# A chunked recurrence cut into two halves of eight heads, with unread products for TensorE

## Chip, cores and metric

The kernel runs on one core of a Trainium2 chip. The metric is the device time of one execution in microseconds (us), the median of several.

## The reference

Two layers, each a recurrent attention and a feed-forward part, on 2 sequences of 1024 tokens with 512 features. The change touches only the attention of the second layer, a test-time-training recurrence over 16 heads of 32 features, in chunks of 16 tokens:

```python
def step(S, inp):                       # S: (B, H, 32, 32), 64 chunks one after the other
    qi, ki, vi, ei = inp
    kh = einsum('bchd,bhde->bche', ki, S)
    target = vi - ki
    mu = mean(kh, -1); rstd = rsqrt(var(kh, -1) + EPS)
    kh_hat = (kh - mu) * rstd
    g = w * kh_hat + b - target
    gw = g * w
    v_new = (gw - mean(gw, -1) - kh_hat * mean(gw * kh_hat, -1)) * rstd
    A = where(tri, einsum('bchd,bshd->bhcs', qi, ki), 0) * ei
    qh = einsum('bchd,bhde->bche', qi, S) - einsum('bhcs,bshe->bche', A, v_new)
    o = qi + _ln(qh, w, b)
    S = S - einsum('bchd,bche->bhde', ki * ei, v_new)
    return (S, o)
```

## The kernel before

The program runs in stages, each closed by a barrier of all engines: the first layer's recurrence, its feed-forward part with the second layer's projections, then `ttt_recurrence` (the stage of the change), attention output, shared experts, routed experts, last stage.

`ttt_recurrence` runs 64 steps (`STEPS`), one for each chunk. All 16 heads and both sequences are done in each: partitions hold 2 sequences x 4 heads x 16 tokens, and the free dimension holds 4 groups `g` of 4 heads. Everything is in float32. In step n:

- TensorE multiplies the next keys (L1343) and these queries (L1350) with the state `S`. It then waits for `u` (the update v_new, scaled) and adds the correction `cross` x `u` to the next keys' product (L1388, so that the next step need not wait for the new state), updates the state in its PSUM bank (L1393), and adds `am` x `u` to the queries' product (L1399). `prepare` (L1357) makes the raw products of keys with queries and with the next keys.
- ScalarE squares the keys' product, takes the root, and copies `S`, `cross` and the result `qh` out of PSUM.
- VectorE does the normalisation and its derivative, a chain of 14 operations that ends in `u` (L1326), then `ub` (L1329, `u` by sequence) and `am` (L1332, masked).
- SP loads the keys and queries (`KQ`), goals (`te`) and keys by row (`kk`) of 8 steps at a time into two buffers, and stores `qh`. GpSimd only clears tiles.

Each engine runs its own order, and semaphores tie them. A float32 matmul stands in the trace as two records, so a block of 8 products has 16.

Of the kernel before, what the change touches and what calls it, by code (L numbers as in the profile page):

```python
# [6 lines left out]
ALU = mybir.AluOpType  # L7
# [6 lines left out]
P = 128  # L14
# [1136 lines left out]
def ttt_recurrence(nc, K, bank, a):  # L1151
# [7 lines left out]
    bS, bQ, bA, bC = bank[0:4]  # L1159
    bH = bank[4:6]  # L1160
    G = KC
# [3 lines left out]
    zero = ph.sb("zero", [P, 2 * P])  # L1165
# [6 lines left out]
    u, ub = ph.sb("u", [P, G, DH]), ph.sb("ub", [P, G, B, DH])  # L1172
    c1, c2, c3, c4, c5, c6 = (ph.sb(f"c{k}", [P, G, DH]) for k in range(6))
    eps, m, re = ph.sb("eps", [P, 1]), ph.sb("m", [P, 6, G]), ph.sb("re", [P, G])
    s = {n: nc.alloc_semaphore(name=f"ttt_{n}") for n in (
        "consts", "zero", "eps", "w2", "s0", "S", "KH", "KS", "QS", "A", "KK", "cross", "sq", "s2", "sd", "xw", "r1", "v1", "rs", "re",
# [13 lines left out]

    def rows(name, i):
        return a[name][i * B * P:(i + 1) * B * P, :]

    with nc.Block() as block:
        @block.sync
        def _(sp):
# [3 lines left out]
            def load(i):  # L1200
                f = i % 2
                if i >= 2:
                    sp.wait_ge(s["QS"], ST * (i - 1))
                    sp.wait_ge(s["KK"], ST * (i - 1))
# [5 lines left out]
                if i >= 2:  # L1210
                    sp.wait_ge(s["u"], ST * (i - 1))
                    sp.wait_ge(s["SU"], ST * (i - 1))
# [8 lines left out]
            def store(i):  # L1221
                sp.wait_ge(s["qh"], ST * (i + 1))
# [20 lines left out]

        @block.scalar
        def _(act):
            nc.scalar.preload_act_table_set("sqrt_and_others")

            def deviation(n):
                act.wait_ge(s["KH"], n + 1)
                if n:  # L1250
                    act.wait_ge(s["r2"], n)
                nc.scalar.activation(c2[:].rearrange("p g e -> p (g e)"), bH[n % 2][:, 0:P], ACT.Square).then_inc(s["sq"], 1)
                act.wait_ge(s["s2"], n + 1)
                nc.scalar.activation(m[:, 2], m[:, 1], ACT.Sqrt, scale=1.0 / DH, bias=eps[:, 0:1]).then_inc(s["sd"], 1)

            def state(n):
                act.wait_ge(s["SU"], n)
                if n:
                    act.wait_ge(s["QS"], n)
                    act.wait_ge(s["KS"], n + 1)  # L1260
                else:
                    act.wait_ge(s["s0"], 1)
                nc.scalar.copy(S[:].rearrange("p g b e -> p (g b e)"), bS[:, 0:2 * P]).then_inc(s["S"], 1)

            state(0)
            act.wait_ge(s["eps"], 1)
            deviation(0)
            for n in range(STEPS):
                f, r = place(n)
                if n + 1 < STEPS:  # L1270
                    act.wait_ge(s["KK"], n + 1)
                    act.wait_ge(s["KH"], n + 1)
# [3 lines left out]
                act.wait_ge(s["AU"], n + 1)  # L1276
                if r == 0 and n >= 2 * ST:
                    act.wait_ge(qh_out[f], 16 * 8 * (n // (2 * ST)))
                nc.scalar.copy(qh[f][:, r].rearrange("p g e -> p (g e)"), bQ[:, 0:P]).then_inc(s["qh"], 1)

        @block.vector
        def _(dve):
            nc.vector.memset(eps[:], 1e-6).then_inc(s["eps"], 1)
# [4 lines left out]
            def over_e(t):  # L1288
                return t.unsqueeze(2).to_broadcast([P, G, DH])

            for n in range(STEPS):
                f, r = place(n)
                kh = bH[n % 2][:, 0:P].rearrange("p (g e) -> p g e", g=G)
                dve.wait_ge(s["sq"], n + 1)
                nc.vector.tensor_reduce(m[:, 1], c2[:], AX, ALU.add).then_inc(s["s2"], 1)
                nc.vector.tensor_tensor(c3[:], kh, w2[:], ALU.mult).then_inc(s["xw"], 1)
                dve.wait_ge(s["xw"], n + 1)
                nc.vector.tensor_reduce(m[:, 4], c3[:], AX, ALU.add).then_inc(s["r1"], 1)
                dve.wait_ge(s["r1"], n + 1)
                nc.vector.scalar_tensor_tensor(c4[:], over_e(m[:, 4]), -1.0 / DH, c3[:], ALU.mult, ALU.add).then_inc(s["v1"], 1)  # L1300
                dve.wait_ge(s["sd"], n + 1)
                nc.vector.reciprocal(m[:, 3], m[:, 2]).then_inc(s["rs"], 1)
                dve.wait_ge(s["v1"], n + 1)
                dve.wait_ge(s["rs"], n + 1)
                nc.vector.tensor_tensor(c3[:], c4[:], over_e(m[:, 3]), ALU.mult).then_inc(s["t"], 1)
                nc.vector.tensor_tensor(c1[:], kh, over_e(m[:, 3]), ALU.mult).then_inc(s["hat"], 1)
                if r == 0:
                    dve.wait_ge(in_te[f], 16 * 16 * (n // (2 * ST) + 1))
                dve.wait_ge(s["t"], n + 1)
                nc.vector.tensor_tensor(c3[:], c3[:], te[f][:, r, :, 0:DH], ALU.add).then_inc(s["gw"], 1)  # L1310
                nc.vector.tensor_tensor(re[:], m[:, 3], te[f][:, r, :, DH], ALU.mult).then_inc(s["re"], 1)
                dve.wait_ge(s["hat"], n + 1)
                dve.wait_ge(s["gw"], n + 1)
                nc.vector.tensor_tensor(c2[:], c3[:], c1[:], ALU.mult).then_inc(s["p"], 1)
                dve.wait_ge(s["p"], n + 1)
                nc.vector.tensor_reduce(m[:, 5], c2[:], AX, ALU.add).then_inc(s["r2"], 1)
                dve.wait_ge(s["r2"], n + 1)
                nc.vector.tensor_tensor(c5[:], c1[:], over_e(m[:, 5]), ALU.mult).then_inc(s["q"], 1)
                dve.wait_ge(s["q"], n + 1)
                nc.vector.scalar_tensor_tensor(c6[:], c5[:], 1.0 / DH, c3[:], ALU.mult, ALU.subtract).then_inc(s["v2"], 1)  # L1320
                if n:
                    dve.wait_ge(s["SU"], n)
                    dve.wait_ge(s["AU"], n)
                dve.wait_ge(s["re"], n + 1)
                dve.wait_ge(s["v2"], n + 1)
                nc.vector.tensor_tensor(u[:], c6[:], over_e(re[:]), ALU.mult).then_inc(s["u"], 1)  # L1326
                dve.wait_ge(s["u"], n + 1)
                if n + 1 < STEPS:
                    nc.vector.tensor_tensor(ub[:], u[:].unsqueeze(2).to_broadcast([P, G, B, DH]),  # L1329
                                            seq[:].unsqueeze(1).unsqueeze(3).to_broadcast([P, G, B, DH]), ALU.mult).then_inc(s["ub"], 1)  # L1330
                dve.wait_ge(s["A"], n + 1)
# [1134 lines left out]
```

## Time and profile before

| | us |
|---|---|
| median of 3 runs | 2649.17 (2643.64 to 2650.5) |
| the profiled execution | 2673.8 |
| its span | 2672.0 |
| mean granted TensorE clock | 0.886 |
| TensorE busy | 2250.8 (84%) |
| VectorE busy | 1544.7 (58%) |
| ScalarE busy | 1116.9 (42%) |
| GpSimd busy | 861.7 (32%) |

The span goes from the first to the last instruction. PE is TensorE's matmul, PEld its weight load, DVE VectorE, ACT ScalarE, POOL GpSimd, SP the queue that issues transfers. PEclk is the clock that TensorE is granted, as a share of 2.4 GHz: 0.50 is 1.2 GHz. Busy shares are averages over stages with different limits, so the recurrence is read by itself.

### The profile page before, as it was taken

To read this page: it belongs to the slowest core of one execution; us is meant where nothing else is said; L and a number is where in the kernel's file an instruction comes from. 1 tells how busy PE (TensorE), PEld (TensorE's weight loads), DVE (VectorE), ACT (ScalarE), POOL (GpSimd) and SP (SyncE) were. 2 spreads that over 40 slices of the span, in tenths; PEclk is the share of its full clock that TensorE was granted. 3 is DMA by queue.
4 is the path that set the end of the run, shared out by engine and by line. 5 is a ranking of instruction groups with operands and counts; after the bars stand their busy time and mean duration, and the time that the engine had idled before them with its cause. 6 is when DMAs were issued, how large, how long until landed. Compare 5 with 4: busy or idle time off the path is not lost. (4 is left out here: it accounts for less than half of the span.)

```text
span 2672.0 us, 59064 instructions
## 1 busy us (share of the span) xinstructions
PE 2250.8 (84%) x23684; PEld 1946.7 (73%) x23684; DVE 1544.7 (58%) x3549; ACT 1116.9 (42%) x2103; POOL 861.7 (32%) x666
## 2 busy tenths in 40 slices
PE   7999983999994999994678994999999999999930
PEld 6778762777773889893446773999999899999930
DVE  4545553555542766666957633656655556655658
ACT  4334332555552322222441111555555555555523
POOL 0000000122211000003410476656665656666621
PEclk9999995888885876777999996999999999999965
DMA  2111103344448354333530002234235523233147
GB/s 106 39 38 38 39 22 118 138 168 178 176 154 205 92 159 105 92 95 117 173 124 12 1 2 94 64 134 140 79 136 190 196 89 139 88 130 133 40 172 284
DMA packets 154572, 300.44 MB, mean 112 GB/s; under 512 B 67097, under 2 KB 93209, under 8 KB 139645
## 3 DMA queue, kind: packets, MB, share of 16 engines
q1 hardware_dynamic: 108285, 181.71, 21.2%
q0 software_dynamic: 44480, 115.41, 12.7%
q8 instruction: 139, 2.28, 0.4%
q10 hardware_dynamic: 1616, 0.62, 0.1%
q14 instruction: 52, 0.43, 0.1%
HBM read 296.72 MB, written 106.27 MB: 151 GB/s over the span
## 5 line engine op out<-in xcount | busy, mean ns | idle before, releaser
L91 PE MATMUL bank<-routed_xh,routed_guh 128*128 128x256 f32 (+1 forms) x1536 | 437.7, 285 | 29.3 <-DVE routed_xl L2171 29.3
L92 PE MATMUL bank<-routed_xh,routed_gul 128*128 128x256 f32 (+1 forms) x1536 | 437.0, 284 | 0.0
L93 PE MATMUL bank<-routed_xl,routed_guh 128*128 128x256 f32 (+1 forms) x1536 | 434.9, 283 | 0.0
L2205 DVE TENSOR_TENSOR routed_gul<-routed_guf,routed_guh 128x2816 fp32r<-128x2816 f32 x64 | 197.9, 3092 | 250.7 <-ACT routed_guh L2148 250.7
L91 PEld LDWEIGHTS bank<-routed_xh,routed_guh 128*128 128x128 f32 (+1 forms) x1536 | 280.5, 183 | 37.7 <-issue 35.3
L2089 POOL DMA_INDIRECT routed_x<-mid_x,routed_xi x132 | 276.5, 2095 | 55.9 <-issue 53.5
L92 PEld LDWEIGHTS bank<-routed_xh,routed_gul 128*128 128x128 f32 (+1 forms) x1536 | 280.2, 182 | 2.0
L93 PEld LDWEIGHTS bank<-routed_xl,routed_guh 128*128 128x128 f32 (+1 forms) x1536 | 281.6, 183 | 0.0
L2098 POOL DMA_INDIRECT mid_y<-routed_y,routed_yi x132 | 138.9, 1052 | 246.7 <-ACT routed_y L2164 224.1
L2158 ACT CAST routed_ih<-routed_sil 128x256 fp32r<-128x256 f32 (+1 forms) x192 | 78.0, 406 | 240.4 <-DVE routed_sil L2210 240.4
L2148 ACT CAST routed_guh<-routed_guf 128x2816 fp32r<-128x2816 f32 x64 | 163.5, 2555 | 35.7 <-DMA routed_guf<-in_GU,routed_wi 35.6
L91 PE MATMUL bank<-routed_dnh,routed_ih 128*128 128x512 f32 (+1 forms) x384 | 157.0, 409 | 0.0
L1887 POOL DMA_INDIRECT mid_slots<-moe_pair,moe_slot x96 | 100.6, 1048 | 173.5 <-DVE moe_slot L1814 144.5
L92 PE MATMUL bank<-routed_dnh,routed_il 128*128 128x512 f32 (+1 forms) x384 | 151.0, 393 | 0.0
L93 PE MATMUL bank<-routed_dnl,routed_ih 128*128 128x512 f32 (+1 forms) x384 | 150.4, 392 | 0.0
L325 POOL TENSOR_TENSOR gla_xt<-gla_xt,gla_shift 128x512 f32<-128x512 f32 x16 | 20.2, 1263 | 342.6 <-DMA gla_xt<-in_x 319.8
L1477 POOL MEMSET out_eps<- 128x1 f32 x1 | 0.1, 98 | 401.2 <-POOLq L83 401.2
L2216 DVE TENSOR_TENSOR routed_il<-routed_sil,routed_ih 128x256 fp32r<-128x256 f32 (+1 forms) x192 | 82.7, 431 | 60.4 <-ACT routed_ih L2158 60.4
L2213 DVE TENSOR_TENSOR routed_dnl<-routed_dnf,routed_dnh 128x1536 fp32r<-128x1536 f32 x64 | 112.2, 1753 | 4.4 <-ACT routed_dnh L2156 4.4
L2164 ACT COPY routed_y<-bank 128x512 f32<-128x512 f32 x128 | 74.3, 588 | 85.9 <-PE bank L93 85.8
L2171 DVE TENSOR_TENSOR routed_xl<-bank,routed_xh 128x512 fp32r<-128x512 f32 x130 | 83.8, 686 | 34.8 <-ACT routed_xh L2135 34.8
L1357 PE MATMUL bank<-ttt_KQ 128*64 128x64 f32 x2032 | 100.4, 273 | 0.0
(456 smaller groups left out, 5780.5 us busy)
## 6 DMA issues: line engine op xcount, KB each, us to landing
last_y<-mid_y SPq DMA_DIRECT2D x16, 1536.0 KB, 9.7
mid_ks<-ffn_kT SPq DMA_DIRECT2D x16, 1024.0 KB
mid_qs<-ffn_qT SPq DMA_DIRECT2D x16, 1024.0 KB
ttt_KQ<-mid_ks SPq DMA_DIRECT2D x16, 1024.0 KB, 6.9
ttt_KQ<-mid_qs SPq DMA_DIRECT2D x16, 1024.0 KB, 12.0
mid_te<-ffn_te SPq DMA_DIRECT2D x16, 264.0 KB, 4.1
ttt_te<-mid_te SPq DMA_DIRECT2D x64, 66.0 KB, 6.0
gla_xT<-in_xT SPq DMA_DIRECT2D x16, 256.0 KB, 3.2
```

Source lines behind the costliest of these rows:

```text
L91: pe.matmul(out, hi(c), whi(c), start=start and c == 0, stop=False, skip_group_check=True)
L92: pe.matmul(out, lo(c), whi(c), start=False, stop=False, skip_group_check=True)
L93: last = pe.matmul(out, hi(c), wlo(c), start=False, stop=stop and c == n - 1, skip_group_check=True)
L1357: last = pe.matmul(out[half(b), g * R64:(g + 1) * R64], keys(n, g, b), other(g, b), start=True, stop=True, skip_group_check=True)
L1887: nc.gpsimd.indirect_dma_start(a["slots"], bass.IndirectOffsetOnAxis(ap=slot6[:, n, j:j + 1], axis=0), pair[:, n, j], None).then_inc(given ...
L2089: nc.gpsimd.indirect_dma_start(x[q][:, h], None, a["x3"], bass.IndirectOffsetOnAxis(ap=xi[q][:, h:h + 1], axis=0)).then_inc(x_in[q], 16)
L2098: nc.gpsimd.indirect_dma_start(a["y"], bass.IndirectOffsetOnAxis(ap=yi[q][:, h:h + 1], axis=0), y[q][:, h], None, bounds_check=B * L * TOP ...
L2148: nc.scalar.copy(guh[q][:].rearrange("p a c n -> p (a c n)"), guf[q][:]).then_inc(s["guh"].sem, 1)
L2171: last = nc.vector.tensor_tensor(xl[q][:, c].rearrange("p c t -> p (c t)"), t_bank[k][:], xh[q][:, c].bitcast(F32).rearrange("p c t -> p ( ...
L2205: nc.vector.tensor_tensor(gul[q][:].rearrange("p a c n -> p (a c n)"), guf[q][:], guh[q][:].bitcast(F32).rearrange("p a c n -> p (a c n)") ...
L2213: nc.vector.tensor_tensor(dnl[r][:].rearrange("p c n -> p (c n)"), dnf[r][:], dnh[r][:].bitcast(F32).rearrange("p c n -> p (c n)"), ALU.su ...
L2216: nc.vector.tensor_tensor(il[r][0:m, c], sil[k][0:m], ih[r][0:m, c].bitcast(F32), ALU.subtract).then_inc(s["il"].sem, 1)
```

## The change

The 4 groups of a step are cut into two halves `h` of 2 groups (eight heads). Every operation of a step is done for each half, with semaphores, PSUM banks and tiles for each. VectorE's order is written out in `both`: the second part of one half's chain takes turns with the first part of the other half's. The product `ub` moves from VectorE to GpSimd. The copies that shared the tiles `c1` to `c6` have tiles of their own, `u` and `ub` are doubled, and the products of keys with next keys go behind the queries' product in its bank.

TensorE gets products that nobody reads, of zeros with zeros in float32r: two of 512 columns that open the state banks, one that opens `bA[0]`, 40 of 512 columns ahead of the wait for the first `KQ`, 8 behind it, and one of 384 columns in each half step between the keys' correction and the state update. They add zeros to banks or parts of banks.

```diff
-    bS, bQ, bA, bC = bank[0:4]
-    bH = bank[4:6]
-    G = KC
+    HALVES, G = 2, KC
+    GH = G // HALVES
+    bS, bQ, bH, bA = bank[0:2], bank[2:4], bank[4:6], bank[6:8]
+    AFTER_Q = GH * DH
...
+            def by_sequence(n, h):
+                pool.wait_ge(done["u"][h], n + 1)
+                nc.gpsimd.tensor_tensor(ub[n % 2][:, heads(h)], u[n % 2][:, heads(h)].unsqueeze(2).to_broadcast([P, GH, B, DH]),
+                                        seq[:].unsqueeze(1).unsqueeze(3).to_broadcast([P, GH, B, DH]), ALU.mult).then_inc(done["ub"][h], 1)
...
             for n in range(STEPS):
-                f, r = place(n)
-                if n + 1 < STEPS:
-                    act.wait_ge(s["KK"], n + 1)
-                    act.wait_ge(s["KH"], n + 1)
-                    nc.scalar.copy(cross[:].rearrange("p g n -> p (g n)"), bC[:, 0:G * R64]).then_inc(s["cross"], 1)
-                    deviation(n + 1)
-                    state(n + 1)
...
+                for h in range(HALVES):
+                    if n + 1 < STEPS:
+                        deviation(n + 1, h)
+                        state(n + 1, h)
+                    result(n, h)
+                    if n + 2 < STEPS:
+                        next_keys(n + 1, h)
...
+            def both(n, h, m, k):
+                to_goal(n, h)
+                rates(n, h)
+                along_keys(n, h)
+                masked(n, h)
+                along_summed(n, h)
+                if m < STEPS:
+                    squares_summed(m, k)
+                projected(n, h)
+                if m < STEPS:
+                    weighted(m, k)
+                taken_off(n, h)
+                if m < STEPS:
+                    weighted_summed(m, k)
+                update(n, h)
+                if m < STEPS:
+                    weighted_centred(m, k)
+                    inverse(m, k)
+                    keys_normed(m, k)
+                    weighted_normed(m, k)
+
+            first_of(0, 0)
+            for n in range(STEPS):
+                both(n, 0, n, 1)
+                both(n, 1, n + 1, 0)
...
+            def prepare(n, h):
                 if n + 1 < STEPS:
+                    if n:
+                        pe.wait_ge(done["qh"][h], n)
...
+            def unread(out, width, n):
+                for _ in range(n):
+                    pe.matmul(out[:, D - width:], still[:, 0:P], still[:, 0:width], start=False, stop=False, skip_group_check=True)
+
+            pe.wait_ge(s["still"], 1)
+            for h in range(HALVES):
+                pe.matmul(bS[h][:], still[:, 0:P], still[:], start=True, stop=False, skip_group_check=True).then_inc(s["s0"], 1)
+            pe.matmul(bA[0][:], still[:, 0:P], still[:], start=True, stop=False, skip_group_check=True)
+            unread(bA[0], D, 40)
             pe.wait_ge(in_KQ[0], 16 * 4)
+            unread(bA[0], D, 8)
+            for h in range(HALVES):
+                keys_times_state(0, h)
+                pe.matmul(bH[h][:, 0:GH * DH], zero[:, 0:P], zero[:, 0:GH * DH], start=False, stop=True, skip_group_check=True).then_inc(done["KH"][h], 1)
+                prepare(0, h)
+            keys_times_state(1, 0)
+            queries_times_state(0, 0)
             for n in range(STEPS):
...
+                for h in range(HALVES):
+                    pe.wait_ge(done["u"][h], n + 1)
+                    if n + 1 < STEPS:
+                        keys_corrected(n + 1, h)
+                        unread(bS[h], D - GH * B * DH, 1)
+                        state_updated(n, h)
+                    queries_corrected(n, h)
+                    m, k = n + h, 1 - h
+                    if m + 1 < STEPS:
+                        keys_times_state(m + 1, k)
+                    if m < STEPS:
+                        queries_times_state(m, k)
+                    if n + 1 < STEPS:
+                        prepare(n + 1, h)
```

## Rows read from the trace of the kernel before

**Rows 1.** The page, part 2: granted TensorE clock in tenths, 40 slices.

```profile
PEclk9999995888885876777999996999999999999965
```

**Rows 2.** Table by stretches of the recurrence; columns are in its first line.

```profile
core 0: us, PE busy (x) PEld busy (x) DVE busy (x) ACT busy (x) POOL busy (x), PEclk, DMA share, GB/s
...
874.00:964.00 90.00, 81.39 (x1820) 76.94 (x1818) 72.27 (x282) 28.18 (x89) 0.00 (x0) 0.92 0.51 128
964.00:997.00 33.00, 33.00 (x485) 31.71 (x482) 18.64 (x71) 6.71 (x21) 0.00 (x0) 0.51 0.31 88
...
1003.00:1037.00 34.00, 34.00 (x488) 32.58 (x489) 20.57 (x80) 7.65 (x24) 0.00 (x0) 0.51 0.24 30
```

**Rows 3.** Timeline, TensorE alone, one step at 1.2 GHz: start, duration, line.

```profile
1013.78 1.01 PE L1343 MATMUL bank<-ttt_S,ttt_KQ 128*64 128x32 f32 x16
1014.60 1.05 PE L1350 MATMUL bank<-ttt_S,ttt_KQ 128*64 128x32 f32 x16
1015.58 1.07 PE L1388 MATMUL bank<-ttt_u,ttt_cross 64*64 64x32 f32 x16
1016.58 1.97 PE L1393 MATMUL bank<-ttt_ub,ttt_kk 128*128 128x64 f32 x8
1018.47 1.07 PE L1399 MATMUL bank<-ttt_u,ttt_am 64*64 64x32 f32 x16
1019.47 1.97 PE L1357 MATMUL bank<-ttt_KQ 128*64 128x64 f32 x32
1021.23 1.01 PE L1343 MATMUL bank<-ttt_S,ttt_KQ 128*64 128x32 f32 x16
```

**Rows 4.** Timeline, TensorE in one step at 2.4 GHz.

```profile
930.22 0.66 PE L1388 MATMUL bank<-ttt_u,ttt_cross 64*64 64x32 f32 x16 [0.61 <-DVE ttt_u L1326]
...
930.81 1.10 PE L1393 MATMUL bank<-ttt_ub,ttt_kk 128*128 128x64 f32 x8
...
935.10 0.66 PE L1388 MATMUL bank<-ttt_u,ttt_cross 64*64 64x32 f32 x16 [0.61 <-DVE ttt_u L1326]
```

**Rows 5.** Timeline, VectorE and ScalarE in that step.

```profile
931.24 0.29 DVE L1295 TENSOR_REDUCE ttt_m<-ttt_c 128x4 f32<-128x128 f32 x1 [0.27 <-ACT ttt_c L1252]
931.44 0.28 DVE L1296 TENSOR_TENSOR ttt_c<-bank,ttt_w 128x128 f32<-128x128 f32 x1
931.55 0.30 ACT L1254 ACTIVATE ttt_m<-ttt_m,ttt_eps 128x4 f32<-128x4 f32 x1 [0.35 <-DVE ttt_m L1295]
...
933.17 0.16 DVE L1311 TENSOR_TENSOR ttt_re<-ttt_m,ttt_te 128x4 f32<-128x4 f32 x1
...
935.08 0.42 DVE L1329 TENSOR_TENSOR ttt_ub<-ttt_u,ttt_seq 128x256 f32<-128x256 f32 x1
```

**Rows 6.** Timeline, the first steps and the last u.

```profile
843.12 0.64 PE L1350 MATMUL bank<-ttt_S,ttt_KQ 128*64 128x32 f32 x16
...
849.32 0.29 DVE L1310 TENSOR_TENSOR ttt_c<-ttt_c,ttt_te 128x128 f32<-128x128 f32 x1 [6.29 <-DMA ttt_kk<-mid_kk]
...
851.09 0.29 DVE L1326 TENSOR_TENSOR ttt_u<-ttt_c,ttt_re 128x128 f32<-128x128 f32 x1
...
851.43 1.07 PE L1388 MATMUL bank<-ttt_u,ttt_cross 64*64 64x32 f32 x16 [7.68 <-DVE ttt_u L1326]
...
1223.05 0.29 DVE L1326 TENSOR_TENSOR ttt_u<-ttt_c,ttt_re 128x128 f32<-128x128 f32 x1
```

**Rows 7.** Timeline, products of 512 columns at 1.2 GHz, ahead of this stage.

```profile
404.27 0.63 PE L92 MATMUL bank<-gla_Wo_hi,gla_yTl 128*128 128x512 f32 x1
404.70 0.63 PE L93 MATMUL bank<-gla_Wo_lo,gla_yTh 128*128 128x512 f32 x1
```

**Rows 8.** Groups of instructions by form, GpSimd: busy us, mean ns.

```profile
L833 POOL TENSOR_TENSOR ffn_te<-ffn_te,ffn_tm 128x512 f32<-128x512 f32 x16 | 16.8, 1048 | 41.8 <-DVE ffn_tm L1033 41.8
...
L820 POOL TENSOR_TENSOR ffn_te<-ffn_kw 128x16 f32<-128x16 f32 x16 | 3.6, 223 | 0.0
```

**Rows 9.** Timeline, TensorE where the clock rises.

```profile
993.16 1.97 PE L1357 MATMUL bank<-ttt_KQ 128*64 128x64 f32 x32
...
996.68 0.65 PE L1388 MATMUL bank<-ttt_u,ttt_cross 64*64 64x32 f32 x16
```

More of the change, by code:

```diff
@@ L1311, in _ @@
[L1311 to L1318, printed above, removed]
@@ L1354, in keys_times, with of, column, keys_times_state @@
-            def keys_times(out, n, other, made):
-                for g in range(G):
+            def of(h):
+                return range(h * GH, (h + 1) * GH)
+            def column(g, width):
+                return slice(g % GH * width, (g % GH + 1) * width)
+            def keys_times_state(n, h):
+                pe.wait_ge(done["S"][h], max(n, 1))
+                if n:
+                    pe.wait_ge(done["hat"][h], n)
+                for g in of(h):
+                    for b in range(B):
+                        last = pe.matmul(bH[h][half(b), column(g, DH)], keys(n, g, b), S[:, g, b, :],
+                                         start=(g == h * GH), stop=False, skip_group_check=True)
+                last.then_inc(done["KS"][h], 1)
@@ new lines, in queries_times_state @@
+            def queries_times_state(n, h):
+                if n + 1 < STEPS:
+                    pe.wait_ge(done["cross"][h], n + 1)
+                else:
+                    pe.wait_ge(done["qh"][h], n)
+                for g in of(h):
+                    for b in range(B):
+                        last = pe.matmul(bQ[h][half(b), column(g, DH)], queries(n, g, b), S[:, g, b, :],
+                                         start=(g == h * GH), stop=False, skip_group_check=True)
+                last.then_inc(done["QS"][h], 1)
@@ L1356, in keys_times @@
+            def keys_times(out, n, h, other, made):
+                for g in of(h):
                     for b in range(B):
-                        last = pe.matmul(out[half(b), g * R64:(g + 1) * R64], keys(n, g, b), other(g, b),
+                        last = pe.matmul(out[half(b), column(g, R64)], keys(n, g, b), other(g, b),
                                          start=True, stop=True, skip_group_check=True)
-                last.then_inc(s[made], 1)
-            def prepare(n):
-                keys_times(bA, n, lambda g, b: queries(n, g, b), "A")
+                last.then_inc(done[made][h], 1)
@@ L1404, in ttt_recurrence, with keys_corrected @@
-    nc.clear_and_free_semaphores([*s.values(), *cleared, *in_KQ, *in_te, *qh_out])
+                    keys_times(bQ[h][:, AFTER_Q:AFTER_Q + GH * R64], n, h, lambda g, b: keys(n + 1, g, b), "KK")
+                keys_times(bA[h], n, h, lambda g, b: queries(n, g, b), "A")
+            def keys_corrected(n, h):
+                pe.wait_ge(done["cross"][h], n)
+                for g in of(h):
+                    for b in range(B):
+                        last = pe.matmul(bH[h][half(b), column(g, DH)], cross[half(b), g, :], u[(n - 1) % 2][half(b), g, :],
+                                         start=False, stop=True, skip_group_check=True)
+                last.then_inc(done["KH"][h], 1)
```

229 lines of the change are left out of this document (122 added, 107 removed).

## Prediction

> **What bounds the kernel now.** I read the page first. The granted clock falls between full and half speed in the slices of 67 us that hold the chunked recurrence [rows 1]. So I cut that stage (about 839 to 1224 us) into stretches of like clock. The reader is to see in [rows 2] that there are two regimes and little between. Where the clock is 0.50 to 0.51, TensorE is busy all of the time (33.00 of 33.00 us, 34.00 of 34.00 us) and VectorE 56 to 60% of it. Where it is 0.92, VectorE is busy 80% and TensorE 90%. I then read one step of each kind. At 0.50 (1.2 GHz) a step is 1021.23 - 1013.78 = 7.45 us, with six TensorE blocks back to back and no wait [rows 3]: TensorE bounds it. At 1.00 (2.4 GHz) a step is 935.10 - 930.22 = 4.88 us, and TensorE waits 0.61 us for u in it [rows 4]. There the bound is the loop u, correction product, Square on ScalarE, the chain of VectorE operations that [rows 5] shows parts of, u again.
>
> From u of step 0 to u of step 63 there are 1223.05 - 851.09 = 371.96 us, or 5.904 us a step [rows 6]. With 4.88 and 7.45 as the two kinds, (5.904 - 4.88) / 2.57 = 0.40 of the steps, 25 of 63, run at 1.2 GHz. So the clock in this stage is worth more (25 x 2.57 = 65 us) than anything that can be hidden at full clock, and the question of the change is which regime it is in.
>
> **The change part by part.** *TensorE's blocks* are cut in two, with the same products in sum. From the starts in [rows 3], at 1.2 GHz: key product with S 0.82, query product with S 0.98, correction by cross 1.00, state update 1.89, query correction 1.00, `prepare` 1.76, in sum 7.45 us. Half a step is 3.72 us.
>
> *The unread product of 384 columns* has no row before. The nearest is a product of 512 columns of the same kind at 1.2 GHz, 404.70 - 404.27 = 0.43 us from start to start [rows 7]; by columns that is 0.43 x 384 / 512 = 0.32 us. Bounds: 0.1 us if most of its stream covers the weight loads around it (the weight load column is as busy as the product column in [rows 2]), 0.55 us if it also exposes a weight load of 0.23 us, which is one product's pitch in the state update (1.89 / 8, [rows 3]). I take 0.32 us, since TensorE's blocks stand back to back and nothing is there to hide it. A half step at 1.2 GHz is then 3.72 + 0.32 = 4.04 us, and a step 8.1 us; I take 8.15 for waits at twice as many seams, with 7.65 and 8.6 as ends.
>
> *VectorE* gets 30 operations a step in place of 16 less ub, half as wide, two chains in turn. An operation of 128 elements takes 0.29 us and lets the next independent one start after 0.20 (931.24 to 931.44, [rows 5]). One of 4 elements takes 0.16 us. So one of 64 takes about 0.22 us. Its pitch lies between 0.13 us (0.20 less 64 elements at the 128-element rate) and 0.20 us. By the lower end, with the 128-wide mask at 0.20, a half step is about 2.2 us, by the upper 3.0 us. At 1.2 GHz both lie under TensorE's 4.04 us and cost nothing.
>
> *ub moves to GpSimd.* A tensor_tensor there takes 0.22 us for 16 elements and 1.05 for 512 [rows 8], so about 0.4 us for 128. It starts when u ends, and TensorE has the correction (0.5 us at 1.2 GHz) and the unread product before it needs ub. Hidden at 1.2 GHz; at 2.4 GHz those two are some 0.3 ((930.81 - 930.22) / 2, [rows 4]) and 0.16 us, so up to 0.1 us may show in a half step. VectorE loses 0.42 us a step [rows 5]. The Trainium skill ("SBUF — State Buffer", section "Who interferes with whom") says that a VectorE instruction with two SBUF inputs and a GpSimd one that reads SBUF lock each other out. By that ub could be late by one VectorE operation more; no row here shows the pair overlapping, and the sum does not use it.
>
> *ScalarE* goes from five operations a step to ten. The one to watch is its order: Square, then the wait for the sum of squares, Sqrt, and behind these the state copy, the result copy and the copy of cross, for all of which TensorE waits (`prepare` for the result). The loop is sum of squares, Sqrt, state copy, result copy, `prepare` of this half, correction of the other half, Square, sum of squares. A ScalarE operation takes about 0.3 us (Sqrt 0.30, [rows 5]), a VectorE one 0.25 with its hand-over, `prepare` of a half 1.76 / 4 = 0.44 at 2.4 GHz and the half correction 0.3 + 0.1 until its reader starts. That makes 0.25 + 3 x 0.3 + 0.44 + 0.4 + 0.3 = 2.3 us a half step, and TensorE's own work is (4.88 - 0.61) / 2 + 0.16 = 2.3 us. With VectorE's 2.2 to 3.0 that makes 2.45 us a half step, 4.9 a step at 2.4 GHz (4.6 to 6.0). That is no better than 4.88: the two halves overlap what was serial, but everything has become as long as the step. At 1.2 GHz its two TensorE terms double, to 3.1 us, under the 4.04.
>
> *SP's queue* only waits on two semaphores for one; its loads are issued eight steps ahead, and nothing else stands behind them.
>
> *The 48 unread products ahead of the first step.* 40 (and 3 that open banks) run after the zeros are there, 8 after KQ has landed. They delay the first key product by at most 8 x 0.43 = 3.4 us, which is hidden: TensorE finishes its work ahead of the loop near 844 us [rows 6], while VectorE can't go on until the last `kk` rows land at 849.3, and u of step 0 is at 851.09. That same wait takes away what they are for. TensorE now runs out of work at about 843.8 and starts again at 851.4; the clock is 0.50 there although it was 1.00 before the pause (843.12: 16 products in 0.64 us; 851.43: 1.07 us). The loads are not changed, so with the new kernel it stands idle at least 4 us at this place and, as here, begins the loop at 1.2 GHz.
>
> **Does the clock rise again?** In the kernel before it does at 996.6, after `prepare` and both products with S had run in one stretch from 993.16; the correction at 996.68 already takes 0.65 us in place of 1.07 [rows 3, 9]. In this stretch a product of 64 columns goes by every 0.055 us (1.76 / 32, [rows 3]); in the state update it is one every 0.24 us, in the corrections one of 32 columns on a quarter of the array every 0.06 us. The same run in the step of 1019.47 brought no rise, so it does not bring one each time. After the change the run is half as long (16 + 8 + 8 products, 1.8 us), and a correction, the state update and a correction stand between two of them. What is added is the unread product, 0.32 us of full-array work in 4.04. It adds to the mean, but it does not replace the long run after which the clock rose. I choose between "rises after some steps" and "never rises" by the row that it is nearest to, the stretches at 0.50 in which TensorE worked all the time [rows 2], and expect the whole loop at 0.50.
>
> **Sum.** 63 x 8.15 = 513.5 against 371.96: +141.5 us. The second half of the last step adds about 2. Nothing else in the program changes. 2673.8 + 143.5 = 2817 us against the profiled execution (span 2672.0 and 1.8 around it). That execution is 24.6 us over the median of 2649.17. If its excess lies elsewhere, the median after is 2793; if it lies in this stage's share of 1.2 GHz, it is 2817. I say 2800; own range 2770 to 2840.
>
> **Rivals.**
> A, the forecast: 1.2 GHz in the whole loop, 2800 us. Chance 0.70.
> B, full clock for (nearly) the whole loop, faster. Place: the first steps after the pause at 851. It decides at a single rise: at 2.4 GHz a half step of 2.45 us leaves no pause of note where there now is one of 0.61 [rows 4], so a clock that has risen may well stay up. One rise in 128 half steps suffices. Price: 63 x 4.9 = 309, -63 us; 2673.8 - 63 = 2611 or, from the median, 2586: 2600 us. For it: the added full-array products; against it: the broken dense run. The Trainium skill ("TensorE: Matmul & The Clock Gate", section "What's actually happening") says that sustained activity releases the throttle; read as busy time, it would give this rival. The trace here speaks against that reading: 33 us and 34 us fully busy at 0.50 to 0.51 [rows 2]. Chance 0.20.
> C, alternating as now, 0.4 of the steps at 1.2 GHz: 0.4 x 8.15 + 0.6 x 4.9 = 6.2 us a step, +19 us: 2668 us. For it: it is what the kernel does now; against it: that the halves make the work even, so that it should stay on one side. Chance 0.07.
> D, full clock, but VectorE's 30 operations at the upper pitch bind at 2 x 3.0 = 6.0 us a step: +6 us, 2655. Chance 0.03.
>
> **How the numbers follow.** A measurement of this kernel tells 0.3% (8 us) from no change. Slower by more: A and most of C, 0.76. Within: D and a little of C, 0.04. Faster: B, 0.20. The predicted time is A's. For 8 in 10 the range must reach into B, since A alone holds 0.7. It goes from 2595, within B, to 2830, a little under A's own end; that leaves out about half of B and a few hundredths of A.
>
> **What would show it.** Right: PEclk 5 in all slices of the recurrence, half steps of about 4.05 us with TensorE always busy, the unread product at a pitch of 0.3 us, VectorE about half busy, ub never waited for; 851 us for the first correction, with a pause ahead of it. Wrong: a rise of the clock after the pause, seen as correction blocks of 8 in 0.3 us; the clock then staying at 1.00; or no pause, should `kk` land earlier. If half steps at 2.4 GHz are much over 2.5 us, the chain on ScalarE (`prepare` behind the result copy) or VectorE's pitch was mis-sized.

## The result, and the profile after it

| | before | after |
|---|---|---|
| median (4 runs each) | 2649.84 us (2643.64 to 2651.82) | 2854.91 us (2850.90 to 2862.91) |
| profiled execution, its span | 2673.8 us, 2672.0 | 2862.91 us, 2861.1 |
| granted clock over the span | 0.886 | 0.829 |
| u of step 0 to last u | 371.96 us | 555.3 us |

The changed kernel is slower: 1.0782 times the time, 95% interval 1.0752 to 1.0812. That is 205 us, where +150 was forecast. Of the profiled difference of 189.1 us the loop holds 183.3; u of step 0 comes 2.8 us later, and from the last u to the end takes 2.9 us more. Here and below, a ratio and its interval leave out executions more than 1.5% above the fastest of the same kernel; medians and ranges hold all of them.

The page after, the granted clock in 40 slices, beside [rows 1]:

```profile
PEclk9999977988975555555589999699999999999975
```

The table by stretches, beside [rows 2]:

```profile
core 0: us, PE busy (x) PEld busy (x) DVE busy (x) ACT busy (x) POOL busy (x), PEclk, DMA share, GB/s
...
852.00:900.00 48.00, 45.85 (x543) 42.14 (x543) 27.20 (x177) 13.61 (x54) 4.39 (x11) 0.50 0.44 105
900.00:1000.00 100.00, 100.00 (x1216) 91.69 (x1215) 53.02 (x340) 28.55 (x113) 9.18 (x23) 0.50 0.33 69
...
1300.00:1400.00 100.00, 100.00 (x1203) 91.80 (x1205) 53.53 (x343) 28.71 (x114) 9.19 (x23) 0.50 0.06 10
```

There is one regime where there were two: 0.50 from end to end, TensorE busy for 100.00 of 100.00 us, VectorE 53%. How the loop begins, from the timeline (start, duration, engine), beside [rows 6]:

```profile
832.70 13.19 PE L1496 MATMUL bank<-ttt_still 128*128 128x512 f32 x48
...
848.45 0.41 PE L1450 MATMUL bank<-ttt_S,ttt_KQ 128*64 128x32 f32 x8
...
852.50 0.23 DVE L1356 TENSOR_TENSOR ttt_gw<-ttt_t,ttt_te 128x64 f32<-128x64 f32 x1 [4.32 <-DMA ttt_kk<-mid_kk]
853.88 0.21 DVE L1380 TENSOR_TENSOR ttt_u<-ttt_v,ttt_re 128x64 f32<-128x64 f32 x1
...
854.15 0.64 PE L1474 MATMUL bank<-ttt_u,ttt_cross 64*64 64x32 f32 x8 [5.29 <-DVE ttt_u L1380]
```

The 48 unread products end at 845.8, and the last work ahead of the loop still runs warm (four float32 products, eight records, in 0.41 us). Then TensorE stands idle for 5.29 us, because VectorE waits 4.32 us for the `kk` load, and the first correction takes 0.64 us: half speed. One half step of the loop, TensorE alone, beside [rows 3]:

```profile
1100.92 0.64 PE L1474 MATMUL bank<-ttt_u,ttt_cross 64*64 64x32 f32 x8
...
1101.49 0.69 PE L1496 MATMUL bank<-ttt_still 128*128 128x384 f32 x1
...
1101.97 0.95 PE L1482 MATMUL bank<-ttt_ub,ttt_kk 128*128 128x64 f32 x4
1102.85 0.64 PE L1490 MATMUL bank<-ttt_u,ttt_am 64*64 64x32 f32 x8
...
1103.42 0.64 PE L1439 MATMUL bank<-ttt_S,ttt_KQ 128*64 128x32 f32 x8
...
1103.87 0.62 PE L1450 MATMUL bank<-ttt_S,ttt_KQ 128*64 128x32 f32 x8
1104.30 1.10 PE L1457 MATMUL bank<-ttt_KQ 128*64 128x64 f32 x16
...
1105.33 0.64 PE L1474 MATMUL bank<-ttt_u,ttt_cross 64*64 64x32 f32 x8
```

No block has an idle time ahead of it. The half step is 4.41 us here and 555.3 / 127 = 4.373 on the mean, where 4.04 (4.075 with its share for waits) was forecast. The first and the last interval between two u are shorter (2.33 and 3.03 us), so the steady half step is the 4.41; steps are compared by it below. The other engines do the waiting. The chain of waits from 860 to 1400 us has none of TensorE (waited for: us in total, times, longest):

```profile
POOL ttt_ub L1257 <- DVE ttt_u L1380: 492.5, 123, 4.0
DVE ttt_am L1384 <- PE bank L1457: 192.2, 122, 1.6
ACT ttt_cross L1291 <- PE bank L1457: 154.2, 122, 1.3
```

The groups of instructions give ub on GpSimd 399 ns (forecast 0.4 us), and the list of u's line gives its first and last start, the measure of the loop used below:

```profile
L1257 POOL TENSOR_TENSOR ttt_ub<-ttt_u,ttt_seq 128x128 f32<-128x128 f32 x126 | 50.3, 399 | 517.9 <-DVE ttt_u L1380 517.9
```

```profile
L1380 DVE TENSOR_TENSOR ttt_u<-ttt_v,ttt_re x128: 211/215/225, 853.9 to 1409.2; 128x64 f32<-128x64 f32 x128
```

### The profile page after: what moved, and what is told of

It is laid out like the page before. It is cut to its first block and busy times, and to the rows that moved or that the text cites. A ratio compares the mean times of both kernels' runs of the same rounds, so it can differ in the third digit from the quotient of the medians.

```text
span 2861.1 us, 60552 instructions
## 1 busy us (share of the span) xinstructions
PE 2475.9 (87%) x23861; PEld 2139.0 (75%) x23861; DVE 1585.1 (55%) x4447; ACT 1176.8 (41%) x2422; POOL 910.0 (32%) x792
## 5 line engine op out<-in xcount | busy, mean ns | idle before, releaser
L1257 POOL TENSOR_TENSOR ttt_ub<-ttt_u,ttt_seq 128x128 f32<-128x128 f32 x126 | 50.3, 399 | 517.9 <-DVE ttt_u L1380 517.9
L1384 DVE TENSOR_TENSOR ttt_am<-bank,ttt_tri 128x128 f32<-128x128 f32 x128 | 37.3, 291 | 196.7 <-PE bank L1457 196.7
L1457 PE MATMUL bank<-ttt_KQ 128*64 128x64 f32 x2032 | 139.2, 317 | 0.0
L1482 PEld LDWEIGHTS bank<-ttt_ub,ttt_kk 128*128 128x128 f32 x504 | 136.0, 332 | 0.0
L1457 PEld LDWEIGHTS bank<-ttt_KQ 128*64 128x64 f32 x2032 | 123.8, 226 | 0.1
L1482 PE MATMUL bank<-ttt_ub,ttt_kk 128*128 128x64 f32 x504 | 119.5, 393 | 0.0
```

The source lines that it names most:

```text
L1457: last = pe.matmul(out[half(b), column(g, R64)], keys(n, g, b), other(g, b), start=True, stop=True, skip_group_check=True)
L1482: last = pe.matmul(bS[h][:, column(g, B * DH)], kk[f][:, r, g].rearrange("p j d -> p (j d)"), ub[n % 2][:, g].rearrange("p b e -> p (b e)" ...
```

## The experiments

They were made in three groups, each on a chip of its own with runs of the kernel before on it: 2651.75 us (12 runs), 2650.13 (11) and, for e9 to e12, 2717.25 (29). On the third chip what lies behind the loop is some 60 us longer (1507.6 to 1513.2 us from the last u to the end, 1449.0 in the first profile), and the loop isn't. So times are compared within a group, and loops across them.

The questions are three. Why does the clock stay down? What does a half step cost at either level? What are the unread products worth?

### e1: fill the pause ahead of the first step

```diff
@@ behind the last product ahead of the loop
+            unread(bS[1], D - GH * B * DH, 36)
```

> The changed kernel with 36 more unread products of 384 columns on TensorE between its last product ahead of the loop and the wait for the first u, so that the 5.3 us pause there is filled. Theory (the clock at which the loop is entered decides, and then stays): the loop begins at 2.4 GHz and the granted clock is 1.00 in all of it; half steps of 2.3 to 2.6 us, so 126 of them take 290 to 328 us in place of 555, and the kernel takes 2590 to 2640 us. Rival 1 (half steps in turns cannot hold 2.4 GHz, however they begin): the clock falls within some steps and the time stays at 2830 to 2870. Rival 2 (the clock alternates as in the kernel before): 2650 to 2750.

Measured: 2786.14 us (2752.59 to 2860.83, 4 runs), ratio 1.045 [1.0363, 1.0536]. The profiled execution is the longest of them:

```profile
844.82 4.67 PE L1496 MATMUL bank<-ttt_still 128*128 128x384 f32 x26
851.39 0.54 PE L1474 MATMUL bank<-ttt_u,ttt_cross 64*64 64x32 f32 x8 [1.90 <-DVE ttt_u L1380]
```

The products ended at 849.5, 1.90 us too early; the correction begins warm (0.54 us for the block, which falls to half speed within it), and from there the loop is 555.2 us, all at 0.50, as in the changed kernel. The other three executions are 72 to 108 us shorter, and their mean granted clock is 0.855 to 0.869 where the profiled one has 0.828, so part of their loops must have been at 2.4 GHz (their loops themselves were not seen). The expected 2590 to 2640 was missed: 36 products don't always fill the pause, and even the best execution stays far over a loop at full clock.

### e2: no product in the half steps; e11: no unread product at all

```diff
@@ e2, in the half step
-                        unread(bS[h], D - GH * B * DH, 1)
@@ e11, that line too, and ahead of the loop
-            unread(bA[0], D, 40)
-            unread(bA[0], D, 8)
```

> The changed kernel without the unread product of 384 columns in each half step; the 48 ahead of the loop stay. Theory (entered at 1.2 GHz, the loop stays there with or without the product, and the product only costs time): clock 0.50 in the whole loop; the half step falls from 4.41 us by the product's 0.48 us less what it hid of the next weight load (0.17), to about 4.1 us, so 126 x 0.31 = 39 us off: about 2816 us. If the product hides nothing: 3.93 us, 2795 us. Rival (the sparse product is what keeps the clock from alternating): alternating clock, under 2750 us.

> The two halves without any unread product, ahead or in the loop, but for the three that open banks. Theory (the loop is entered at 1.2 GHz through the pause anyway, and stays): clock 0.50 in the whole loop, half steps of 4.08 us, 2816 us as without the products in the loop. Rival (the 48 products ahead do something for the loop): a time over 5 us away from 2816.

Measured: e2 2816.44 us, e11 2883.4 on the third chip (one run each); their loops are both 515.0 us (u from 856.9 to 1371.9 and from 853.4 to 1368.4), all at 0.50. e2 met the expected 2816. e11 lies 67 us over it, and all of that is behind the loop, which takes 1513.2 us to the end there and 1442.7 in e2. TensorE in e2:

```profile
1102.41 0.64 PE L1474 MATMUL bank<-ttt_u,ttt_cross 64*64 64x32 f32 x8
1102.98 1.11 PE L1482 MATMUL bank<-ttt_ub,ttt_kk 128*128 128x64 f32 x4
1104.02 0.64 PE L1490 MATMUL bank<-ttt_u,ttt_am 64*64 64x32 f32 x8
1104.59 0.64 PE L1439 MATMUL bank<-ttt_S,ttt_KQ 128*64 128x32 f32 x8
...
1106.50 0.64 PE L1474 MATMUL bank<-ttt_u,ttt_cross 64*64 64x32 f32 x8
```

Two things follow. The 48 products ahead of the loop change nothing in it. And the unread product costs 4.41 - 4.09 = 0.32 us a half step at 1.2 GHz, as forecast (by the loops, (555.3 - 515.0) / 127 = 0.317). It stands for 0.48 us in the changed kernel's timeline, but the state update behind it is shorter for it (0.88 us there, 1.04 here). What is left is 2 x 4.09 = 8.18 us a step with the same products as 7.45 in [rows 3]. So 0.73 us a step come from cutting the blocks in half.

### e7: the two corrections side by side

```diff
                     if n + 1 < STEPS:
                         keys_corrected(n + 1, h)
+                    queries_corrected(n, h)
+                    if n + 1 < STEPS:
                         unread(bS[h], D - GH * B * DH, 1)
                         state_updated(n, h)
-                    queries_corrected(n, h)
```

> The changed kernel with the queries' correction directly behind the keys' correction, ahead of the unread product and the state update; nothing is added or left out. In its trace a pair of products follows the last at 0.107 us in a block, but at 0.22 to 0.35 us where the shape of the tile changes (128x64, 64x64, 128x128), four times in a half step. Theory (the change of shape costs this): one change fewer, the half step goes from 4.41 to about 4.29 us, 126 x 0.12 = 15 us less, about 2840 us, at 0.50 throughout. Rival (the waits on semaphores at the blocks' starts cost it): the waits are the same in number, 4.41 us and 2855 us.

Measured: 2830.92 us (one run; 2840 was expected), loop 537.7 at 0.50.

```profile
1102.61 0.64 PE L1474 MATMUL bank<-ttt_u,ttt_cross 64*64 64x32 f32 x8
1103.06 0.62 PE L1490 MATMUL bank<-ttt_u,ttt_am 64*64 64x32 f32 x8
1103.61 0.69 PE L1496 MATMUL bank<-ttt_still 128*128 128x384 f32 x1
1104.09 0.95 PE L1482 MATMUL bank<-ttt_ub,ttt_kk 128*128 128x64 f32 x4
```

The key correction now takes 0.45 us (1102.61 to 1103.06) and not 0.57, with the same four products (eight records). Behind it stands a block of its own tile shape (64\*64, the pair printed after the names) and not one of 128\*128. The loop is 17.6 us shorter, 0.14 us a half step. The waits are all still there, so it isn't they that cost: it is each change of tile shape between one product and the next. Where a wait stands and the shape stays, nothing shows: the two blocks with S follow each other after 0.45 and 0.43 us, the pace of their products. The single records of e2 and e7 say the same: from one pair of records to the next it is 0.100 us within most of a block and equally from block to block where the shape stays, but 0.221 or 0.244 us where it changes, and 0.351 us from the state update, whose own pitch is 0.213 to 0.266, to the next shape. The kernel before has four such changes in a step, the halves without the product have eight, and (8.18 - 7.45) / 4 = 0.18 us each. The Trainium skill ("TensorE: Matmul & The Clock Gate", section "Step-by-step: what each phase is for") says that a weight load is pulled ahead of running products where their row groups don't conflict, or where it goes to the background weight buffer. A change of shape that stands in the way of that could be the reason; no run here separates it from another one.

### e3 and e5: the pause filled, none or one product in the half steps

```diff
@@ e3: 36 in the pause, none in the half step
+            unread(bS[1], D - GH * B * DH, 36)
-                        unread(bS[h], D - GH * B * DH, 1)
@@ e5: 54 in the pause, one in the half step as in the change
+            unread(bS[1], D - GH * B * DH, 54)
```

> The changed kernel with the pause filled by 36 unread products of 384 columns, and without the product in each half step. Theory: TensorE is fed well enough by the half steps themselves, the clock stays at 1.00, and the time is that of the kernel with filled pause or up to 20 us less (126 x 0.16 us at most). Rival (the product in each half step is needed to hold the clock): stretches at 0.50 in the loop, 30 us or more above the kernel with filled pause.

> As the kernel with filled pause, but with 54 products in the pause, since 36 ended 1.9 us before the first u. Theory: the loop now begins at 2.4 GHz; with the product in each half step it stays there longer than without it (which was until a 1.6 us halt of TensorE at 947 us), perhaps to the end: 126 half steps of 2.5 us = 315 us, so about 2600 to 2615 us if it stays. If a halt still ends it, all after that is at 0.50 and the time lies between, by 1.9 us for each half step left. Rival (the clock falls without a halt): falls at places that differ from run to run with no idle time before them.

Measured: e3 2748.26 us (2745.98 to 2827.33, 4 runs), ratio 1.0344 [1.0272, 1.0416]; e5 2762.53 (2759.86 to 2763.69, 4 runs), 1.0409 [1.0362, 1.0457]. TensorE and two stretches of e3, and the like of e5:

```profile
946.27 0.55 PE L1482 MATMUL bank<-ttt_ub,ttt_kk 128*128 128x64 f32 x3
948.43 0.48 PE L1482 MATMUL bank<-ttt_ub,ttt_kk 128*128 128x64 f32 x1 [1.61 <-issue]
...
860.00:947.00 87.00, 86.81 (x1899) 78.79 (x1895) 82.54 (x550) 41.34 (x183) 14.47 (x37) 1.00 0.58 139
949.00:1290.00 341.00, 341.00 (x4350) 310.74 (x4352) 194.81 (x1245) 105.41 (x417) 33.10 (x83) 0.50 0.31 73
```

```profile
1001.02 0.40 PE L1450 MATMUL bank<-ttt_S,ttt_KQ 128*64 128x32 f32 x8
1002.91 0.69 PE L1457 MATMUL bank<-ttt_KQ 128*64 128x64 f32 x16 [1.48 <-issue]
...
1005.00:1300.00 295.00, 295.00 (x3552) 270.75 (x3551) 157.12 (x1006) 84.50 (x335) 26.71 (x67) 0.50 0.27 64
```

This is the run pair that shows both levels in one loop. With the pause filled (in e3 0.53 us of it were left) the halves run at full clock: 2.37 us a half step in e3, 2.55 in e5, TensorE busy 86.81 of 87.00 us. Then TensorE halts, 1.61 or 1.48 us in the middle of its work, with "issue" and no other engine as its releaser (e5 has one more halt, of 0.7 us at 910, behind which the clock stays up). The clock falls to 0.50, and from there it stays at 0.50 for 341 and 295 us of unbroken work. Loops: 448.4 us in e3, 458.3 in e5. The same code runs at either level in one execution, and which one depends on what it came in with. e3's theory (the clock stays at 1.00) failed, and so did its rival: in e5 the product stood in each half step and the clock fell all the same. For e5 its second branch came, a halt and 0.50 from there. One of e3's four executions, 2827.33 us at a mean clock of 0.831, is 79 us longer than the others (0.860 to 0.862); it must have fallen much earlier.

### e8: five products in each half step; e6: a burst in every eighth step

```diff
@@ e8
-                        unread(bS[h], D - GH * B * DH, 1)
+                        unread(bS[h], D - GH * B * DH, 5)
@@ e6, with the 54 of e5 in the pause
-                        unread(bS[h], D - GH * B * DH, 1)
+                        unread(bS[h], D - GH * B * DH, 12 if n % 8 == 7 and h == 0 else 1)
```

> The changed kernel with five unread products of 384 columns in each half step in place of one. At 1.2 GHz that is 4 x 0.32 = 1.28 us more in each, so if the loop stays at 0.50 (rival: what is added cannot bring the clock back) the half step is 5.7 us and the time 2855 + 161 = 3016 us. Theory (it is full-array work in a run that is missing; with enough of it the clock rises within the first steps and stays): clock 1.00, TensorE bounds the half step at 2.4 + 5 x 0.16 = 3.2 us, so 126 x 3.2 = 403 us in place of 555: about 2700 us, faster although more is done.

> As the kernel with the longer fill, but in every eighth step the first half step has 12 unread products of 384 columns in place of one: 8 x 11 x 0.16 to 0.32 us = 14 to 28 us of work more. Theory (dense work brings the clock back, so that a fall costs at most eight steps): the clock is 1.00 in most of the loop, and the time is 2610 to 2650 us, in all runs. Rival (once at 1.2 GHz, the loop stays there whatever is added): as the kernel with the longer fill plus 14 to 28 us.

Measured: e8 2724.97 us (one run); e6 2664.05 (2652.46 to 2698.85, 8 runs), ratio 1.0029 [0.9984, 1.0073]. TensorE in e8, with a stretch of 100 us, and in e6:

```profile
870.43 1.97 PE L1496 MATMUL bank<-ttt_still 128*128 128x384 f32 x5
872.20 0.81 PE L1482 MATMUL bank<-ttt_ub,ttt_kk 128*128 128x64 f32 x4
872.94 0.42 PE L1490 MATMUL bank<-ttt_u,ttt_am 64*64 64x32 f32 x8
...
900.00:1000.00 100.00, 100.00 (x1753) 93.28 (x1750) 72.30 (x462) 39.03 (x154) 12.38 (x31) 1.00 0.47 118
```

```profile
1120.34 3.34 PE L1496 MATMUL bank<-ttt_still 128*128 128x384 f32 x12
1123.52 0.55 PE L1482 MATMUL bank<-ttt_ub,ttt_kk 128*128 128x64 f32 x4
```

e8 does more work than the changed kernel in every half step, with the same kind of pause ahead of the loop (5.93 us idle), and takes 130 us less (about 2700 was expected): after some 20 us at half speed (5.69 us a half step) the clock rises in the state update at 872.20, and the rest of the loop, 418.4 us in all, is at 1.00. In e6 the clock fell after a halt of 1.78 us at 1092, stayed down for some 27 us, and came back within a burst: twelve products in 3.2 us, and the state update behind them already in 0.49. So full-array products do bring the clock back; one of 384 columns in a half step did not in the 295 us of e5. e6's executions missed the 2610 to 2650 expected of all of them, and by its interval it can't be told from the kernel before.

### e12: the pause filled, three in each half step

```diff
@@ with the 54 of e5 in the pause
-                        unread(bS[h], D - GH * B * DH, 1)
+                        unread(bS[h], D - GH * B * DH, 3)
```

> The halves with the longer fill (54 products in the pause) and three products of 384 columns in each half step. Theory (enough to outlast the halts of TensorE of 1.5 to 2 us, which ended 2.4 GHz with none and with one product): clock 1.00 to the end of the loop, half steps of 2.55 + 2 x 0.16 = 2.88 us, 363 us in place of 555: 2640 to 2665 us. Rival (three are not enough to outlast a halt, or to come back from one): 0.50 from some halt on, with half steps of 5.05 us, and 2700 us or more.

Measured: 2732.92 us (2726.16 to 2737.17, 10 runs), ratio 1.0057 [1.0029, 1.0086], loop 368.6 at 1.00 throughout:

```profile
1000.00:1100.00 100.00, 100.00 (x1898) 92.53 (x1894) 80.69 (x517) 43.58 (x173) 13.63 (x34) 1.00 0.52 138
```

A half step is 368.6 / 127 = 2.90 us, the forecast 2.88. (The expected 2640 to 2665 us were meant for a chip that does the kernel before in 2650; 1.0057 times that is 2665.) Held at full clock from end to end, the halves are no faster than the kernel before with its mix of both levels, 0.6% slower by the medians: the products that hold it there cost what it brings, and there is no idle time of TensorE left for them to lie in (100.00 of 100.00 us).

### e4, e9, e10: whole steps with unread products

The kernel before, with 100 products of 256 columns ahead, 62 in the pause, and three (e4), six (e9) or none (e10) in each step just before the wait for u, where [rows 4] have 0.61 us of idle time:

```diff
+            def unread(n):
+                for _ in range(n):
+                    pe.matmul(bank[6][:, 2 * P:], still[:, 0:P], still[:, 0:2 * P], start=False, stop=False, skip_group_check=True)
...
+            unread(100)
...
+                unread(62 if n == 0 else 3)
```

> The kernel before, its steps whole, with the unread products alone: 100 of 256 columns ahead of the first keys, 62 in the pause before the first u, 3 in each step where TensorE waits for u, all into a bank that nothing uses. Theory (clock and halves are separate; the products fill the wait for u of 0.61 us in a 4.88 us step): clock 1.00 in the whole loop, 63 steps of 4.9 us = 309 us in place of 372, so 63 us less: 2585 to 2600 us. Rival (the whole step has a stretch too sparse to hold the clock, whatever the products): alternating clock with steps of 4.9 and 8.1 us, 2640 to 2700 us.

> The kernel before, steps whole, with 100 products ahead, 62 in the pause, and six of 256 columns in the wait for u of each step in place of three. With three its step was 4.88 us at 2.4 GHz, and the profile still showed the clock at 0.50 for 3.4, 13.7 and 34 us, each after a halt of TensorE of 1.2 to 1.8 us. Theory (more full-array work in the step brings the clock back sooner after a halt): fewer or shorter stretches at 0.50, 63 steps of 4.9 to 5.0 us, 2600 to 2625 us. Rival (six no longer fit in the wait and lengthen the step by more than they give back): 2630 to 2660 us.

> The kernel before with the 100 products ahead and the 62 in the pause alone, none in the steps. Theory (the clock of whole steps does not depend on how they were entered, since they lose and regain it by themselves): within 10 us of the kernel before, 2640 to 2655 us. Rival (the clean start is what gave the gain of 23 us): 2620 to 2635 us.

Measured: e4 2628.4 us (2613.39 to 2656.05, 9 runs), ratio 0.9905 [0.9856, 0.9954]; e9 0.9953 [0.9921, 0.9986] (12 runs) and e10 0.9959 [0.9925, 0.9993] (10 runs) on the third chip. All three gains are under 2%, but their intervals lie below 1. Two steps' ends and three stretches of e4:

```profile
873.21 0.65 PE L1397 MATMUL bank<-ttt_u,ttt_cross 64*64 64x32 f32 x16
...
877.40 0.62 PE L1372 MATMUL bank<-ttt_still 128*128 128x256 f32 x3
878.09 0.66 PE L1397 MATMUL bank<-ttt_u,ttt_cross 64*64 64x32 f32 x16
...
925.00:1038.00 113.00, 109.81 (x2446) 100.92 (x2444) 94.33 (x367) 36.45 (x115) 0.00 (x0) 1.00 0.62 152
1040.00:1053.00 13.00, 13.00 (x172) 12.28 (x173) 8.25 (x32) 2.75 (x9) 0.00 (x0) 0.50 0.16 27
1055.00:1160.00 105.00, 103.05 (x2279) 94.48 (x2275) 87.94 (x341) 34.27 (x108) 0.00 (x0) 1.00 0.49 118
```

The step is 4.88 us with the three products as without them [rows 4]: they lie wholly in the wait for u. The clock still falls at halts (1.34 us at 916, 0.95 us at 1036), but these steps bring it back by themselves, within 4 and 14 us. What the products in the steps do is seen beside e10, where the pause is filled and the waits for u are not:

```profile
860.02 0.66 PE L1397 MATMUL bank<-ttt_u,ttt_cross 64*64 64x32 f32 x16 [0.61 <-DVE ttt_u L1328]
...
861.64 0.92 PE L1408 MATMUL bank<-ttt_u,ttt_am 64*64 64x32 f32 x16
```

Here the clock falls at 861.9, within the second of these blocks, with no halt ahead of it, only the ordinary wait of 0.61 us. It falls 18 times in this loop, and in the 7 us ahead of 16 of these falls no idle time is over 0.62 us. In e4 and e9, whose waits hold products, it falls twice and once, each time behind a halt of 0.95 us or more. So in these executions whole steps lose the clock at their ordinary waits, and with products in the waits they keep it; whether the filled time or the full-array work does it, no run separates.

Profiled loops: 319.0 us (e4, at 0.97 on the mean from 856 to 1175), 330.9 (e9, 0.99) and 340.6 (e10, 0.84), against 371.96, which belongs to an execution 24 us over its median. Six products don't fit in the wait: e9's step is 5.10 us, 0.22 longer, some 14 us in the loop, which is what its rival had. The expected 2585 to 2600 for e4 was missed by a loop of 319 for 309 us, and because the 372 us that it was to replace were those of the long execution. e10 gains 11.5 us by its medians, more than its theory allowed (10) and less than its rival (15 to 30). e4 is 1% faster than the kernel before. How much of that is due to the three products in the steps isn't settled by the medians: its executions differ by 43 us, e9 and e10 have all but the same intervals, and e4 ran on another chip.

## Why the prediction was wrong in size and right in mechanism

The case that was forecast, A, came, but the time lies outside its own range of 2770 to 2840 and outside the stated range of 2595 to 2830.

**Right: the loop is entered at 1.2 GHz and never leaves it.** The idle time was forecast as at least 4 us and measured 5.29, and e11 with e2 show that the 48 products do nothing. "Never rises" was chosen by the row that it was nearest to, TensorE busy all of the time at 0.50 [rows 2], and not derived; it held for 555 us. The reason given, that the one product does not replace a long dense run, agrees with e8 and e6, where five and twelve products brought the rise. (The pitches given there, 0.055 and 0.24 us, are those of records, two to a product.) The Trainium skill's rule ("TensorE: Matmul & The Clock Gate", section "What's actually happening") that sustained activity releases the throttle, read as busy time, is contradicted by that stretch. Its section "HAM oscillation — how this bites in real kernels", by which an idle gap throttles the engine again, agrees with the pause. That the clock also fell behind idle times of 1.48 to 1.90 us (e1, e3, e5) and behind waits of 0.61 us (e10), shorter than the gaps that section speaks of, it does not have; here the runs decide.

**Right: the unread product (0.32 forecast, 0.32 by e2), ub (0.40 and 0.399), and all that was costed at nothing.** VectorE is 53% busy, an operation of 64 elements takes 0.21 to 0.23 us, GpSimd, ScalarE and VectorE wait and nobody waits for them. SP's queue shows nowhere.

**Wrong: "I take 8.15 for waits at twice as many seams, with 7.65 and 8.6 as ends".** This step of the sum failed. A steady step took 2 x 4.41 = 8.82 us (8.75 on the mean), outside the ends. It is 7.45 for the products, 0.64 for two unread ones, and 0.73 for the seams, for which 0.07 was allowed. Seams were thought of as waits, and satisfied waits cost nothing. What costs is the change of tile shape, four times a step before and eight times now, 0.14 (e7) to 0.18 us (e2) for each one more, at 1.2 GHz. The timeline of [rows 3] had it already: 1013.78 to 1014.60 for a block of sixteen records with the same shape behind it is 0.82 us, and 1014.60 to 1015.58 for sixteen like them with another shape behind is 0.98. The 0.16 between them is the price. I had read it as a property of the query product and halved it with the rest. By it the term would have been 7.45 + 0.64 + 4 x 0.16 = 8.73.

By the profiled executions: forecast 2817.3, measured 2862.9, of the difference 39.8 from the loop to its last u (183.3 less 143.5; its last half step took 3.0 us where 2 were put down) and 5.7 from its two sides. The median after is 55 us over the forecast: these 45.6, and 17.3 from choosing 2800 and not 2817, less the 8.0 by which the profiled execution of after lies over its median. The medians differ by 205 us and the profiled executions by 189, so most of the 24 us by which the profiled execution of before lies over its median belonged to what the change replaces. I argued both ways and took the middle. That the excess lay in the loop's share of 1.2 GHz is borne out by the granted clocks of the kernel before in e5's group: 0.901 in its shortest execution (2640.26 us), 0.886 in its longest (2669.18). Eleven steps more at 1.2 GHz would do just that, by an estimate from [rows 3] and [rows 4] (28 us more, a mean of 0.887). No trace of a shorter execution was taken.

**The rival at full clock** was mis-priced as well as unlikely. Its half step is 2.55 us and not 2.45 (e5). And "one rise in 128 half steps suffices" is wrong: a halt of TensorE undoes it, and with one product in the half step the clock did not come back (e5, 295 us). Where it is held, three products must pay for it, and the kernel is 0.6% slower than before (e12).

## What to carry to other kernels

Count the changes of tile shape between neighbouring matmuls before cutting a block of them in two; here a satisfied wait on TensorE showed no cost, a change of shape 0.14 to 0.18 us at 1.2 GHz. A stage of narrow products can be fully busy and sit at half clock for good, so ask what it enters with and what could bring it back, and put unread full-array products first where TensorE waits anyway (e4). Where it is the bound they can bring back a lost clock (e8 beats the changed kernel by 130 us), but they cost what it brings: neither e8 nor e12 beats the kernel before. Work ahead of a pause of 5 us did not protect the clock through it; only work in the pause did, and it had to last nearly to its end (e1 missed it by 1.90 us and lost the clock, e3 by 0.53 and kept it).

## What the runs showed of the hardware that was not expected

**The level is remembered.** The same half steps ran for 87 us at 1.00 and then for 341 us at 0.50 (e3), with TensorE busy all of the time at both.

**TensorE halts at full clock.** Besides those in e3, e5 and e6 (1.61, 1.48, 1.78 us), the kernel before has some; its chain of waits from 855 to 1222 us (us in total, times, longest) names them:

```profile
PE bank L1388 <- issue: 2.0, 1, 2.0
PE bank L1343 <- issue: 1.1, 2, 0.9
PE bank L1350 <- issue: 0.9, 1, 0.9
```

The view of the changed kernel from 860 to 1400 us has none at 0.50, and neither have e8 and e12 from 860 to the loop's end. The trace names no releaser for a halt, but it does show what stands ahead: the program's instructions come in blocks of 16 KB by DMA queue q8, which take about 1.0 to 1.2 us (medians by run), and each of the halts with "issue" of 0.9 us or more in e3, e4, e5, e6, e9 and e10 begins between 0.1 us before and 1.1 us after the landing of a block that took 1.4 to 2.4 us (in the kernel before, two of three do). In e5 the block goes from 999.73 to 1001.44 and the halt begins at 1001.43, at the end of a load of `te` and `kk`. That points at instructions that come late behind the loads. It isn't shown: e12 and e8 have blocks as slow and no such halt, and no run changes the loads alone. Nor does the length of a halt alone decide the clock: it fell behind one of 0.95 us (e4) and stayed up behind ones of 1.08 (e9) and 1.16 us (e6). In e3 and e5 it was such a halt that ended a clock which the halves could not regain. e5's four executions lie within 3.8 us of each other, and a half step at the one level costs 4.41 - 2.55 = 1.9 us more than at the other, so in all of them the fall should have come at nearly the same half step.

**Chips differ behind the loop.** On the third chip the part from the last u to the end took 60 us more, while the loop of e11 was the same 515.0 us as that of e2 on another.
